# Row gathers of a mixture-of-experts block issued nine tiles ahead in place of six

## The reference, cut to what matters

```
probs = softmax(x @ gate_w.T);  topk_w, topk_idx = top_k(probs, 6);  topk_w /= sum(topk_w)
combine = sum(one_hot(topk_idx, 64) * topk_w)                  # 64 experts, 6 a token
h = silu(einsum('th,eih->tei', x, experts_w1))                 # 176 hidden values an expert
y = einsum('tei,ehi->teh', h, experts_w2)
out = layernorm(x + einsum('teh,te->th', y, combine) + shared_out)
```

## Time and profile before

| what | value |
|---|---|
| time, median of 3 runs | 1293.59 us (1291.06 to 1298.01) |
| the profiled execution's own time | 1297.3 us |
| its span, first to last instruction | 1295.6 us |
| mean granted clock of TensorE | 0.95 |
| PE busy, share of the span | 1128.8 us, 87% |
| DVE | 825.3 us, 64% |
| ACT | 633.3 us, 49% |
| POOL | 592.2 us, 46% |
| first PE instruction of the experts' block | at 907.78 us |
| last `down` of the experts' block starts | at 1237.10 us |

### The profile page before, as it was taken

One profiled execution on the slowest core, in us unless ns is written; L12 is line 12 of the kernel. 1 busy time (PEld: TensorE's weight loads), 2 busy tenths in 40 slices (PEclk: granted clock), 3 DMA queues, 4 the chain that ended last, 5 costly groups with the idle time before them and its releaser, 6 DMA issues. The chain is left out here.

```text
span 1295.6 us, 21119 instructions
## 1 busy us (share of the span) xinstructions
PE 1128.8 (87%) x6374; PEld 660.5 (51%) x6374; DVE 825.3 (64%) x1537; ACT 633.3 (49%) x1320; POOL 592.2 (46%) x589
## 2 busy tenths in 40 slices
PE   5489999999999995888898977897999998999965
PEld 2152222222222223455753556356888886788854
DVE  6399999999999945665454556897333333222246
ACT  1126777777777781455313342221555554444471
POOL 7000355667345363576541102458544457555521
PEclk8888999999999997999989997899899999999989
DMA  4990234234130104000000000210689888788877
GB/s 135 152 228 14 47 59 64 28 41 61 27 44 13 13 9 171 0 2 1 1 3 1 1 1 10 89 56 26 197 242 242 238 238 252 241 267 255 261 253 253
DMA packets 128383, 137.21 MB, mean 106 GB/s; under 512 B 47430, under 2 KB 99366, under 8 KB 128207
## 3 DMA queue, kind: packets, MB, share of 16 engines
q1 hardware_dynamic: 118783, 110.42, 34.2%
q0 software_dynamic: 9216, 25.18, 6.1%
q10 hardware_dynamic: 272, 0.26, 0.1%
HBM read 109.06 MB, written 24.12 MB: 103 GB/s over the span
## 5 line engine op out<-in xcount | busy, mean ns | idle before, releaser
L495 ACT ACTIVATE l_ret_store<-attn_st 128x512 f32<-128x512 f32 x512 | 280.1, 598 | 103.1 <-PE attn_st L406 93.3
L519 DVE TENSOR_REDUCE attn_neg<-attn_mx 128x8 f32<-128x1024 f32 x256 | 299.2, 1202 | 12.9 <-PE attn_mx L386 11.9
L2010 DVE SCALAR_TENSOR_TENSOR exp_sums<-exp_y_ps,moe_mask,exp_sums 128x256 f32 x159 | 77.0, 484 | 202.8 <-PE exp_y_ps L1921 97.3
L406 PE MATMUL attn_st<-attn_q_st,attn_k_st 128*128 128x512 bf16 x512 | 173.9, 384 | 2.8 <-ACT l_ret_store L495 2.1
L1912 PE MATMUL exp_h_ps<-keep_prod,moe_w 128*88 128x128 f32 x1272 | 169.9, 277 | 7.1 <-DMA moe_w<-in_w 5.2
L386 PE MATMUL attn_mx<-attn_k_st,attn_q_st 96*128 96x512 bf16 x512 | 156.2, 387 | 14.5 <-DVE attn_neg L519 14.2
L1912 PEld LDWEIGHTS exp_h_ps<-keep_prod,moe_w 128*88 128x88 f32 x1272 | 147.8, 158 | 23.6 <-DMA moe_w<-in_w 12.2
L418 PE MATMUL attn_o<-l_ret_store,l_ret_tab 128*32 128x512 f32 x1024 | 136.4, 604 | 0.8 <-ACT l_ret_store L495 0.8
L1874 POOL DMA_INDIRECT y_rows<-exp_sums,moe_dst_i x96 | 93.7, 976 | 82.9 <-DVE exp_sums L2010 75.6
L406 PEld LDWEIGHTS attn_st<-attn_q_st,attn_k_st 128*128 128x128 bf16 x512 | 48.3, 97 | 155.9 <-ACT l_ret_store L495 114.6
L1966 ACT ACTIVATE moe_ht<-exp_h_ps 88x256 f32<-88x256 f32 x159 | 60.4, 380 | 95.6 <-PE exp_h_ps L1912 95.5
(11 more groups left out here) (317 smaller groups left out, 1921.0 us busy)
## 6 DMA issues: line engine op xcount, KB each, us to landing
moe_w<-in_w SPq DMA_DIRECT2D x254, 176.0 KB
keep_prod<-in_w SPq DMA_DIRECT2D x64, 176.0 KB
exp_tiles<-y_rows SPq DMA_DIRECT2D x11, 768.0 KB, 10.3
parts<-l0b_front SPq DMA_DIRECT2D x32, 192.0 KB, 10.6
attn_k_st<-parts SPq DMA_DIRECT2D x48, 128.0 KB, 7.1
attn_q_st<-parts SPq DMA_DIRECT2D x48, 128.0 KB, 7.7
l_ret_tab<-in_tables SPq DMA_DIRECT2D x4, 1024.0 KB
exp_sums<-y_rows SPq DMA_DIRECT2D x5, 768.0 KB, 10.5
```

What stands on the lines that cost most here:

```text
L406: pe.matmul(st_ps[n % BANKS][:], k_st[g % BUFS][:, h, kt * P:(kt + 1) * P], q_st[g % BUFS][:, h, c * CH:(c + 1) * CH], start=True, stop=Tr ...
L495: act.activation(probs[s % 2][:, h], st_ps[n % BANKS][:], ACT.Exp, scale=SCALE0).then_inc(exp_done, 1)
L519: dve.tensor_reduce(neg[m % 2][:, i], mx_ps[slot["score", n] % 2][:].rearrange("p (j k) -> p j k", k=P), AX.X, ALU.max, negate=True).then_ ...
L2010: dve.scalar_tensor_tensor(out=sums[:, bass.ds(at, 1)], in0=y_ps[b % 2][:, 0:E].unsqueeze(1), scalar=mask[:, b:b + 1], in1=sums[:, bass.ds ...
```

## The change

In `experts`, POOL issues `gather(6)`, `gather(7)` and `gather(8)` before its loop, and slot b of the loop then holds `gather(b + 9)` in place of `gather(b + 6)`. The number of gathers and scatters, the buffers, all waits and all other engines stay as they are. `LEAD` is 6 and `RB` is 9.

```
+            for t in range(LEAD, RB):
+                gather(t)
             for b in range(STEPS):
-                if b + LEAD < FULL:
-                    gather(b + LEAD)
+                if b + RB < FULL:
+                    gather(b + RB)
                 if b >= EXPERTS:
                     scatter(b - EXPERTS)
             scatter(FULL - 1)
```

## The result

The changed kernel takes 1284.5 us in the median of 20 runs (1280.5 to 1292.7), the kernel before 1294.3 us in the 20 runs beside it (1287.3 to 1300.6). The ratio is 0.9932, interval 0.9916 to 0.9949: 8.8 us less by the ratio (9.8 by the two medians), where 6.7 were forecast. All runs of the experiments further down together put the gain at 6.4 us: sets of runs of one and the same program differ by more than such an interval.

A forecast was written before the change was run, and what follows sets the result against it. POOL's 2.57 us a slot against PE's 1.96 a step was taken as the bound. Earlier gathers gain 7.7 us, the ring of sums takes back 1.0: 1293.6 - 6.7 = 1286.9 us, own range 1285 to 1289, wider range 1282.5 to 1295.

The forecast's parts named there:

- What bounds the stage: Gathers and scatters alternating: POOL needs 2.57 us a slot, PE 1.96 a step; PE waits for rows, 14.5 us lost.
- The three gathers ahead of the loop: Before POOL's loop: issuing them there changes nothing, since slots 0 to 2 already held just these gathers without waits or scatters.
- Step 1: POOL's last gather, tile 95, moves from slot 89 to 86 and gains 7.7 us; last turn at 1105.1.
- Step 2: Ring of sums: DVE's memset waits for the scatter of slot 86, so `down(92)` comes 1.0 us later, leaving 6.7.
- Step 3: Stage after the last gathers: order and pace as now, no change; six scatters back to back cost 0 to 1, taken 0.
- The DMA side: Weights, gathers and scatters together need 286 GB/s, a DMA share of 0.93; whether weights slow was left open.
- C: Rival: weights' landing binds in the gather-and-scatter stage; some 3 us of gain, 1290.5, or none, 1293.6; chance 0.20.
- E: Rival: weights landing in 7.6 us on average make the stage slower by 6.5 us, 1300.1; chance 0.06.
- D: Rival: the gain is lost in the later stage, bound by SP and the weights; 1293.6; chance 0.09.
- B: Rival: the ring of sums never binds or gathers land faster; full 7.7 us or a little more, 1285.9; chance 0.15.
- A: The forecast: POOL's order gives 7.7 us, the ring takes back about 1; gain 5.7 to 7.5; chance 0.50.
- What I said the profile would show: Experts' block: first scatter about 1044.5, last gather 1099.8, last turn near 1105, PE's row waits from 14 us to 7.

The follow-up runs named there:

- ring68: Changed kernel with the rings of tiles and sums holding 68 in place of 70: 1292.2 us, ratio to the kernel before 0.999.
- lead12: Changed kernel with twelve row buffers and gathers twelve ahead in place of nine, rings still of 70: 1287.6 us, ratio to the kernel before 0.9962.
- lead11_ring72: Changed kernel with gathers eleven ahead in place of nine and rings of 72 in place of 70: 1282.4 us, ratio to the kernel before 0.9922.
- late9: Changed kernel written with no gathers ahead of the loop and gathers 70 to 73 together in slot 64, same instruction order: 1290.8 us, ratio 0.999.
- after: The changed kernel itself, gathers nine ahead in place of six in the kernel before: 1284.5 us, ratio 0.9932.
- late9_again: Repeat of late9, unchanged: 1288.2 us, ratio to the kernel before 0.9951.
- after_again: Repeat of the changed kernel, unchanged: 1290.5 us, ratio to the kernel before 0.9956.
- before_again: The kernel before, unchanged, timed against itself as if it were a change: 1293.8 us, ratio 0.9995.

## Why the prediction held, point by point

**What bounds the stage.** Right: POOL's 2.57 us a slot against PE's 1.96. The series 69.4, 67.1, 63.9, 61.8 for leads of 6 to 9 shows it, beside a spread of 0.9 us between the two profiles of before.

**The three gathers ahead of the loop: nothing.** Right by the order of the instructions; no run tests it by itself. The way from the first matmul to the first scatter is 1.3 to 4.1 us longer in the four profiles of the changed program than in the two of before. In the mean that is about 3 us, of which 2.3 lie between the turns of tiles 10 and 61, where the instructions are the same. Two profiles of before are few, and the cause stays open. The later extra gathers, of tiles 71 to 73, fell into POOL's idle time as said. Did they hurt the weights there? From the turn of tile 61 to that of tile 67 the two profiles of before show 12.1 and 13.1 us, the four of the changed program 13.7, 12.8, 14.1 and 12.3: 0.6 us more in the mean, and within the spread.

**Step 1, the last gather.** Right to 0.1 us: 55.3 behind the first scatter. Its landing was taken as 5.23, and the median became 5.2. The last turn comes 60.6 us behind the first scatter (1100.21 - 1039.58), as forecast (1105.1 - 1044.5), though it stands there behind a `down` that the ring held.

**Step 2, the ring of sums.** Right in place and in kind, and ring68, lead12 and lead11_ring72 show that it is a bound. Its size was a little off: the landing of 4.8 was the median, but the way from the landing to `down` is 0.76, not 1.27, since the add stands directly behind the memset where both are late. The forecast stretch was 62.7 (1107.2 - 1044.5); the four profiles show 61.8, 61.9, 63.6 and 62.0. In all four `down(92)` starts 0.76 or 0.77 us behind the memset that waited for the scatter of slot 86, and what differs is the landing of that one scatter, 4.45, 4.58, 6.26 and 4.66 us: late9's long stretch is one late landing.

**Step 3, the stage behind it.** About right. From `down(92)` to the block's last row of PE the two profiles of before show 123.2 and 123.3 us, the four of the changed program 122.6, 124.0, 125.0 and 123.8, on average 0.6 more; over all twelve kernels with a longer lead it is 122.2 to 126.6. Whether the scatters in a row beside the weights cost about this, as I had allowed for, two profiles of before can't tell; it stays open.

**The DMA side, and C and E.** They fell as what sets the time, but the weights did not stay free. The weight loads of `up` waited twice in after's stage, 0.2 us each time, and lead11_ring72 carries 291 GB/s at a share of 0.93 with PE full. In the repeats PE itself waited more, as late9 from 1041.88 to 1105.49 us shows:

```profile
PE exp_h_ps L1917 <- DMA moe_w<-in_w: 0.8, 2, 0.6
PE exp_h_ps L1917 <- DMA keep_prod<-in_w: 0.5, 2, 0.3
```

It was 1.0 us in late9_again, none in after_again, and none in this stage in the two profiles of before. The rule that all issuing engines share the same DMA engines (the Trainium skill, DMA: Bandwidth & Descriptors, "Issuing engines are not separate DMA queues") agrees with what the landings did: 4.5 to 5.2 us for gathers and 4.3 to 4.8 for scatters, in the median. The repeats bear this out, with 5.3 to 5.5 and 4.8 to 5.1, where before_again has 4.3 for both. The price was in those landings, and for the weights at most 1.3 us, far from what I read out of the rule, rival C with some 3 us of gain: all runs together gained 6.4.

**D** fell: the stage after moved along with its start. **B** can't be told from A by the size: against the first profile of before three of the four stretches came within 0.1 to 0.3 us of the full 7.7 (69.4 - 7.7 = 61.7), but against the mean of both profiles the mean gain is 6.6. As a mechanism, that the ring never binds, B is wrong: ring68 and the waits of `down` for DVE show it.

**What I said the profile would show** named positions, and these hold only from the first scatter on, since the block began 6.3 us earlier. It had one plain error: that PE's waits for rows would go from 14 to 7 us. They went to 1.3. By my own step 2 it had to be so: where the scatter's path is the later one, the rows are already there, and the waiting moves to `down`. The 7 us are right as PE's whole loss (6.9).

**The size.** Forecast 6.7 us; 8.8 in the first comparison, 6.4 over all runs, 7.6 between the first two profiles' stretches and 6.6 between the means (68.9 for the two of before, 62.3 for the four). The first result, 1284.5 us, lies just outside the forecast's own range of 1285 to 1289, on the side of B. That the mean gain comes within 0.3 us of the forecast is in part luck: one landing moved a stretch by 1.6 us or more, and the two terms of step 2, a hand-over taken 0.5 too long and a landing that was 0.2 longer in the mean of the four, partly cancelled.

## What to carry to other kernels

When one engine issues two kinds of transfers in turn, what a longer lead gains is its number of slots, and it ends where the other kind becomes the one that is late. Follow the second kind's release (here a ring that must be written out before it is cleared) to the same slot before counting the gain, and move both bounds together. For a few us in a thousand, compare a stretch of the trace that one engine paces, and time the same program twice before believing an interval.

## What the runs showed of the hardware that was not expected

One program, timed in four sets of 10 to 20 runs, gave medians from 1284.5 to 1290.8 us and ratios from 0.9932 to 0.999, two of which have intervals that don't meet. The same 51 steps of unchanged work took 102.1 to 108.6 us from profile to profile, between the extremes mostly through waits for weights.

POOL's issue was steady in comparison: in the stage with both, a gather or a scatter every 1.28 to 1.29 us in every profile, so that the last gather stood 55.30 to 55.36 us behind the first scatter in all six profiles with nine tiles of lead. The DMA share was 0.81 to 0.94 in the rows shown of this stage.
